# State-space scan on one core: three PSUM banks for the decay arguments, one for y

## The chip, the core and the metric

The kernel runs on one core of a Trainium2 chip. The metric is the device time of one execution in microseconds; a smaller number is better. TensorE (PE) multiplies, ScalarE (ACT) applies functions and copies, VectorE (DVE) does the elementwise work, GpSimd (POOL) builds small operands, and SyncE (SP) issues the transfers.

## The reference

A small vision tower: patch embedding of 64 images into 37 tokens of width 256, then four residual blocks (a selective state-space block, a mixture of experts, a latent attention, a second mixture of experts), each behind a layer norm. The change is in the scan of the first block, which is, cut to what matters:

```python
delta = softplus(x @ W_delta + b_delta)
dA  = exp(delta[..., None] * A)                            # 64 images x 128 channels x 64 states, per token
dBx = delta[..., None] * Bm[:, :, None, :] * x[..., None]
def step(h, inputs):
    dA_t, dBx_t, C_t = inputs
    h = dA_t * h + dBx_t
    y_t = einsum("bdn,bn->bd", h, C_t)
    return h, y_t                                          # 37 steps, one per token
```

## The kernel before

**The state.** The state of one token step is 128 partitions by 4096 words (32 pairs of images by 128 channels). A ring of eight such states lies in SBUF (`slot`). The 37 steps t are worked off in halves: a step has four groups m = 0 to 3 of 1024 words, and each half (m = 0, 1 or m = 2, 3) handles its even group on one path and its odd group on another.

**The even group** (m = 0, 2). DVE multiplies decay and old state (`decay_state`, L1850), PE puts the injected term dBx into PSUM banks 2 and 3 (`inject`, by `inject_rows`, L1088), DVE adds it (`add_injected`, L1869).

**The odd group** (m = 1, 3). DVE writes decay times old state into PSUM banks 4 and 5 (`seed_state`, L1858), PE accumulates the injected term on it (`grow`, also L1088), and ACT copies the two banks to SBUF (`copy_grown`, L1572). The next half's `seed_state` waits for that copy, since it writes the same two banks.

**The decays.** For every four steps (a block; nine of them, b = 0 to 8) PE computes the arguments delta times A as 32 quads, each four matmuls into one bank (`make_quad`, L1081), and ACT exponentiates each quad into the decay slots of the coming block (`exp_quad`, L1548). The quads of block b are spread over 13 group positions of block b-1, from m = 3 of its first step on: two after each even group and three after each odd one (`quads_made`). So a loaded half holds two quads (m even), then the grow and its copy, then three quads (m odd). They use banks 0 and 1 in turn: quad k waits for the exponential of quad k-2. The first exponential of a block overwrites states, and so also waits for DVE's multiplications and seeds of the block's first step, and the first `decay_state` of a block waits for all 32 exponentials.

**The output.** `read_state` (L1121, eight matmul records each) multiplies the state of a half with windows of C that POOL builds. Two steps make one y block, which accumulates in bank 6 or 7 in turn. It waits for the half's add and for its copies. ACT evicts the block (`evict_rows`, L1557), PE transposes it back into the first 128 columns of the same bank (`turn_y`, L1130), and ACT copies the result to y (`copy_y`, L1564).

**Order.** Every engine works its own list in a fixed order written out by hand. PE: inject or grow, then read_state (m even), then turn_y (m = 3 of odd t), then the quads of this position. ACT, at each position: copy_grown (m odd), evict_rows (m = 1 of odd t), copy_y (m = 0 of even t), then the exponentials. DVE: decay, two seeds, add. The semaphores `decay_ps` and `decayed` count quads made and exponentiated; SP's reloads of delta wait on `decay_ps`.

Of the kernel before, what the change touches and what calls it, by code (L numbers as in the profile page):

```python
# [12 lines left out]
P = 128  # L13
# [24 lines left out]
NYB = (L + 1) // 2  # L38
assert NBLK * BLK == L - 1
# [59 lines left out]
def build(nc, small, dense, patches, w_lin, a_rows, up0, dn0, w1, w2, b1, b2, gates_dram, slots,  # L99
          rows_dram, delta_dram, h_dram, gate_dram, out):  # L100
    with ExitStack() as ctx:
# [199 lines left out]
        decay_ps, decayed = sem("decay_ps"), sem("decayed")  # L301
# [3 lines left out]
        y_evicted, y_turned, y_copied = sem("y_evicted"), sem("y_turned"), sem("y_copied")  # L305
# [411 lines left out]

        RANGES = ((0, 9, 0, 4), (9, L, 4, THALF))
# [5 lines left out]
        def _(sp):  # L724
# [54 lines left out]
            def load_delta(b):  # L779

                if b >= 2:
                    sp.wait_ge(decay_ps, QUADS * (b - 1))
# [46 lines left out]
            sp.wait_ge(decay_ps, QUADS * NBLK)  # L829
# [159 lines left out]
        def _(pe):  # L989
# [86 lines left out]
            def make_quad(b, k):  # L1076

                g, r = k // 2, k % 2
                pe.wait_ge(decayed, QUADS * b + k - 1)
                for e in range(4):  # L1080
                    mm = nc.tensor.matmul(ps[:, r, e * BT:(e + 1) * BT], a_stat[64 * r:64 * r + 64, g, e, :],  # L1081
                                          delta_in[b % 2][64 * r:64 * r + 64, g, :], start=True, stop=True)
                mm.then_inc(decay_ps, 1)
# [8 lines left out]
            def inject(t, m):  # L1092

                if m == 0:
                    pe.wait_ge(inject_in[t % INJ], 16 * 9 * (t // INJ + 1))
                pe.wait_ge(added, 2 * t + m // 2)
                inject_rows(t, m, 0, 2, True)
                inject_rows(t, m, 1, 3, True).then_inc(injected, 1)

            def grow(t, m):  # L1100

                for half in range(2):
                    if t >= 1:
                        pe.wait_ge(seeded, 4 * (t - 1) + m - 1 + half + 1)
                    elif m == 3:
                        pe.wait_ge(copied, half + 1)
                    inject_rows(t, m, half, 4 + half, t == 0).then_inc(grown, 1)

            def read_state(t, r):
# [6 lines left out]
                if first and yb >= 2:  # L1116
                    pe.wait_ge(y_copied, yb - 1)
                for j in range(4):
                    quad = r * 4 + j
                    win = t % SLOTS * 256 + quad * 32  # L1120
                    mm = nc.tensor.matmul(ps[32 * j:32 * j + 32, 6 + yb % 2, :], c_win[:, win:win + 32],  # L1121
                                          slot[slot_of(t)][:, quad * 512:(quad + 1) * 512],
                                          start=first, stop=(tp == 1 and r == 1), skip_group_check=True)
                mm.then_inc(read_ps, 1)

            def turn_y(yb):

                pe.wait_ge(y_evicted, yb + 1)
                for x in range(4):
                    mm = nc.tensor.matmul(ps[:, 6 + yb % 2, 0:P], y_rows[yb % 2][:, x * P:(x + 1) * P],  # L1130
                                          S("turn")[:, x * P:(x + 1) * P], start=(x == 0), stop=(x == 3))
                mm.then_inc(y_turned, 1)
# [3 lines left out]
            for k in range(QUADS):  # L1136
                if k < 2:
                    pe.wait_ge(piece_cut, 6 + 2 * k + 1)
                    g, r = k // 2, k % 2
                    for e in range(4):  # L1140
                        mm = nc.tensor.matmul(ps[:, r, e * BT:(e + 1) * BT], a_stat[64 * r:64 * r + 64, g, e, :],
                                              delta_in[0][64 * r:64 * r + 64, g, :], start=True, stop=True)
                    mm.then_inc(decay_ps, 1)
# [314 lines left out]
        def _(act):  # L1458
# [86 lines left out]
            def exp_quad(b, k):  # L1545

                act.wait_ge(decay_ps, QUADS * b + k + 1)
                nc.scalar.activation(decay_slots[b % 2][:, :, 4 * k:4 * k + 4],  # L1548
                                     ps[:, k % 2, :].rearrange("p (e t) -> p t e", e=4),
                                     ACT.Exp).then_inc(decayed, 1)  # L1550

            def evict_rows(yb):

                act.wait_ge(read_ps, 4 * yb + 2)
                if yb >= 2:
                    act.wait_ge(y_turned, yb - 1)
                nc.scalar.activation(y_rows[yb % 2], ps[:, 6 + yb % 2, :], ACT.Copy).then_inc(y_evicted, 1)  # L1557

            def copy_y(yb):

                act.wait_ge(y_turned, yb + 1)
                got = ps[:, 6 + yb % 2, 0:P].rearrange("p (i l) -> p i l", i=NI)
                n = 1 if yb == 0 else 2
                nc.scalar.activation(y3[:, :, max(2 * yb - 1, 0):2 * yb + 1], got[:, :, 2 - n:2],  # L1564
                                     ACT.Copy).then_inc(y_copied, 1)

            def copy_grown(t, m):

                for half in range(2):
                    act.wait_ge(grown, 4 * t + m - 1 + half + 1)  # L1570
                    quad = 2 * m + half
                    nc.scalar.activation(slot[slot_of(t)][:, quad * 512:(quad + 1) * 512], ps[:, 4 + half, :],  # L1572
# [163 lines left out]
        def _(dve):  # L1736
# [106 lines left out]
            def decay_state(t, m):  # L1843

                if m == 0 and (t - 1) % BLK == 0:
                    dve.wait_ge(decayed, QUADS * (block_of(t) + 1))
# [5 lines left out]
            def seed_state(t, m):  # L1852

                now, before = slot[slot_of(t)], slot[slot_of(t - 1)]
                for half in range(2):
                    hs = slice((2 * m + half) * 512, (2 * m + half + 1) * 512)
                    dve.wait_ge(copied, 4 * (t - 1) + m - 1 + 2 + half + 1)
                    nc.vector.tensor_tensor(ps[:, 4 + half, :], now[:, hs], before[:, hs],  # L1858
                                            ALU.mult).then_inc(seeded, 1)

            def add_injected(t, m):
# [3 lines left out]
                if t == 0:  # L1865
                    nc.vector.tensor_copy(now, ps[:, 2:4, :]).then_inc(added, 1)
                else:
                    dve.wait_ge(multed, 2 * (t - 1) + m // 2 + 1)
                    nc.vector.tensor_tensor(now, now, ps[:, 2:4, :], ALU.add).then_inc(added, 1)  # L1869
# [9 lines left out]
            dve.wait_ge(y_copied, NYB)  # L1879
# [351 lines left out]
```

## Time and profile before

| what | value |
|---|---|
| time, median of 3 runs | 1216.77 us (1213.23 to 1216.87) |
| the profiled execution, own time | 1216.49 us |
| its span | 1214.3 us |
| mean granted TensorE clock | 0.862 of full |
| busy over the span | PE 82%, DVE 54%, ACT 42%, POOL 24% |
| the scan | from 154 to 564 us of the span |

Busy shares are over the whole span. An engine's idle time is listed with the work whose end released it. In a timeline, "x8" are eight instructions merged into one row, and the bracket is the idle time before the first of them. The duration of a merged row runs from its first start to its last end, and neighbouring instructions of an engine overlap in part.

### The profile page before, as it was taken

How to read it: one execution, taken by the hardware profiler on the slowest of the kernel's cores; microseconds unless marked ns; L12 is line 12 of the kernel's file. 1: busy time of each engine (PE TensorE's matmuls, PEld its weight loads, DVE VectorE, ACT ScalarE, POOL GpSimd, SP SyncE). 2: the span in 40 equal slices, each digit the busy share in tenths (PEclk: the TensorE clock that was granted, in tenths of full speed). 3: DMA queues.
4: the chain of work that ended last, by engine and by line, in shares of the span. 5: the costliest groups of instructions: out<-in, count | busy, mean ns of one | idle time of the engine just before them, and what ended most of it. 6: DMA issues, size and time to landing. Idle time of an engine off the chain costs nothing.

```text
span 1214.3 us, 17630 instructions
## 1 busy us (share of the span) xinstructions
PE 991.2 (82%) x5925; PEld 614.1 (51%) x5926; DVE 658.1 (54%) x1129; ACT 515.7 (42%) x1028; POOL 295.5 (24%) x361
## 2 busy tenths in 40 slices
PE   8986272777877878765999999998999999559996
PEld 6763230332232333222567777775776666336664
DVE  1544722577676667777535444444876676413332
ACT  1237360766576666662432222224444443223332
POOL 5904901122222222100000000004543541141222
PEclk9998655767677677798989999999999999759999
DMA  5292479212112211116153121100000000342221
GB/s 222 87 335 92 110 211 214 50 44 45 43 27 44 44 26 42 30 38 280 70 218 114 40 73 47 40 0 1 1 1 1 0 1 1 139 160 75 86 78 35
DMA packets 92705, 96.06 MB, mean 79 GB/s; under 512 B 64350, under 2 KB 78687, under 8 KB 90976
## 3 DMA queue, kind: packets, MB, share of 16 engines
q1 hardware_dynamic: 89904, 87.91, 23.7%
q0 software_dynamic: 2736, 7.30, 1.6%
q8 instruction: 39, 0.64, 0.2%
q14 instruction: 26, 0.21, 0.1%
HBM read 61.57 MB, written 34.59 MB: 79 GB/s over the span
## 4 chain that ended last, share of the span: by engine, by line
PE 66%; ACT 14%; DVE 7%; issue 4%; DMA 4%; SPq 4%; POOL 2%; ACTq 0%; DVEq 0%; POOLq 0%
PE ps L524 8%; PE ps L583 7%; PE ps L1121 7%; ACT mem L1548 6%; PE ps L1003 4%; PE ps L1405 4%; PE ps L1421 4%; PE ps L1081 4%; ACT mem L1572 3%; PE ps L1316 3%; PE ps L393 3%; PE ps L1250 3%; PE ps L401 2%; PE ps L1088 2%; PE ps L1130 2%
## 5 line engine op out<-in xcount | busy, mean ns | idle before, releaser
L1548 ACT ACTIVATE mem<-ps 128x512 f32<-128x512 f32 x288 | 160.2, 607 | 104.0 <-PE ps L1081 78.6
L1081 PE MATMUL ps<-mem 64*128 64x128 bf16 x1144 | 106.7, 257 | 98.7 <-ACT mem L1548 96.5
L960 POOL TENSOR_TENSOR mem<-mem,sm 128x296 f32<-128x296 f32 x128 | 87.7, 720 | 361.8 <-ACT mem L1637 319.1
L1081 PEld LDWEIGHTS ps<-mem 64*128 64x128 bf16 x1144 | 63.0, 109 | 195.9 <-ACT mem L1548 166.2
L938 POOL TENSOR_SCALAR mem<-mem,sm 128x16 f32<-128x16 f32 x148 | 92.0, 645 | 274.6 <-PE ps L1121 274.6
L1858 DVE TENSOR_TENSOR ps<-mem 128x512 f32<-128x512 f32 x144 | 93.6, 695 | 61.4 <-ACT mem L1572 61.2
L524 PE MATMUL ps<-mem 128*128 (+1 forms) x384 | 111.6, 422 | 0.6 <-DVE mem L497 0.6
L1121 PE MATMUL ps<-mem 128*32 128x512 f32 x592 | 107.9, 809 | 2.3 <-issue 1.6
L1850 DVE TENSOR_TENSOR mem<-mem 128x1024 f32<-128x1024 f32 x72 | 87.7, 1218 | 35.6 <-ACT mem L1548 35.6
L1572 ACT ACTIVATE mem<-ps 128x512 f32<-128x512 f32 x148 | 82.2, 605 | 58.3 <-PE ps L1088 58.1
L1088 PE MATMUL ps<-mem 64*128 64x512 bf16 x296 | 89.7, 487 | 15.8 <-DVE ps L1858 7.2
L1869 DVE TENSOR_TENSOR mem<-mem,ps 128x1024 f32<-128x1024 f32 x72 | 87.6, 1217 | 27.3 <-PE ps L1088 27.3
L583 PE MATMUL ps<-mem 128*128 128x296 f32 x352 | 99.7, 413 | 2.2 <-DVE mem L646 2.2
L607 ACT ACTIVATE mem<-ps 128x296 f32<-128x296 f32 x88 | 36.7, 417 | 141.9 <-PE ps L524 137.9
L524 PEld LDWEIGHTS ps<-mem 128*128 128x128 f32 x384 | 74.5, 194 | 24.4 <-issue 1.6
L583 PEld LDWEIGHTS ps<-mem 128*128 128x128 f32 x352 | 66.8, 190 | 23.4 <-DVE mem L646 2.6
L646 DVE TENSOR_TENSOR mem<-mem 128x296 f32<-128x296 f32 x88 | 41.1, 467 | 41.8 <-ACT mem L607 39.6
L640 DVE TENSOR_TENSOR mem<-mem 128x296 f32<-128x296 f32 x64 | 29.9, 467 | 52.2 <-ACT mem L607 46.8
L1405 PE MATMUL ps<-mem 128*128 x104 | 51.4, 617 | 7.6 <-issue 7.0
L1003 PE MATMUL ps<-mem 128*128 128x288 f32 x192 | 51.9, 425 | 5.2 <-DMA mem<-in_patches 5.2
L1088 PEld LDWEIGHTS ps<-mem 64*128 64x128 bf16 x296 | 23.7, 107 | 62.8 <-DVE ps L1858 43.3
L431 DVE TENSOR_TENSOR mem<-mem 128x592 f32 (+1 forms) x32 | 25.0, 781 | 49.2 <-ACT mem L418 49.2
(224 smaller groups left out, 1617.5 us busy)
## 6 DMA issues: line engine op xcount, KB each, us to landing
mem<-gates SPq DMA_DIRECT2D x7, 1184.0 KB, 6.0
mem<-in_w SPq DMA_DIRECT2D x2, 4096.0 KB, 17.7
slots<-mem SPq DMA_DIRECT2D x1, 6682.0 KB, 23.8
mem<-slots SPq DMA_DIRECT2D x26, 257.0 KB, 2.7
mem<-in_patches SPq DMA_DIRECT2D x7, 864.0 KB, 4.6
mem<-factor_rows SPq DMA_DIRECT2D x296, 16.0 KB, 1.8
mem<-factor_rows SPq DMA_DIRECT2D x37, 128.0 KB, 2.3
mem<-delta_rows SPq DMA_DIRECT2D x9, 512.0 KB, 4.5
```

What stands on the lines that cost most here:

```text
L524: mm = nc.tensor.matmul(ps[:, bank, 0:CH], w[:, k, row0:row0 + P], xn[:, k, cols], start=(k == 0), stop=(k == HALVES - 1))
L583: mm = nc.tensor.matmul(ps[:, 1 + 2 * cj + m, 0:CH], dn_w[:, j - 2, m * P:(m + 1) * P], hid2[:, b, :], start=(j == 2 and n == nt), stop=(j ...
L938: nc.gpsimd.tensor_scalar(c_win4[:, t % SLOTS * 2 + r, :, w0:w0 + 8].rearrange("p j (x i) -> p j x i", i=2)[:, :, :, i], c_all[:, r * 16:r ...
L960: last = nc.gpsimd.tensor_tensor(kbd[p % 2][:, a, im, :, :], bc(kT[cj][:, a, t0:t0 + L], 1, 8), bc(mask, 2, L), ALU.mult)
L1003: mm = nc.tensor.matmul(ps[:, 2 * j + m, 0:IC * NP], wl[:, f, m * P:(m + 1) * P], xin[:, j, f, :], start=(f == 0), stop=(f == FK - 1))
L1081: mm = nc.tensor.matmul(ps[:, r, e * BT:(e + 1) * BT], a_stat[64 * r:64 * r + 64, g, e, :], delta_in[b % 2][64 * r:64 * r + 64, g, :], sta ...
L1088: return nc.tensor.matmul(ps[:, bank, :], b_in[t % INJ][rows, m, :], dx_in[t % INJ][rows, m, :, :].rearrange("p x n -> p (x n)"), start=st ...
L1121: mm = nc.tensor.matmul(ps[32 * j:32 * j + 32, 6 + yb % 2, :], c_win[:, win:win + 32], slot[slot_of(t)][:, quad * 512:(quad + 1) * 512], s ...
L1405: mm = nc.tensor.matmul(ps[:, 2 + j, 0:HID1], slot_xT[j][:, k, :], w1s[:, k, ds(e * HID1, HID1)], start=(k == 0), stop=(k == 1))
L1548: nc.scalar.activation(decay_slots[b % 2][:, :, 4 * k:4 * k + 4], ps[:, k % 2, :].rearrange("p (e t) -> p t e", e=4), ACT.Exp).then_inc(de ...
L1572: nc.scalar.activation(slot[slot_of(t)][:, quad * 512:(quad + 1) * 512], ps[:, 4 + half, :], ACT.Copy).then_inc(copied, 1)
L1858: nc.vector.tensor_tensor(ps[:, 4 + half, :], now[:, hs], before[:, hs], ALU.mult).then_inc(seeded, 1)
```

## The change

The eight banks are dealt out anew. The quads of decay arguments go round banks 0, 1 and 2; the injected term moves to banks 3 and 4, the grown group to 5 and 6, and y accumulates in bank 7 alone. The transposed y no longer goes back into its own bank but takes a place in the ring of three, in the order in which quads and y blocks come (`RING_AT`). Two semaphores count places instead of quads: `made` (by PE) and `taken` (by ACT, raised by the exponentials and by copy_y). A place waits for the place three before it. On ACT, evict_rows stands ahead of copy_grown at m = 1 of odd t, and copy_y moves from m = 0 of the next step to m = 3 of the same step, behind copy_grown. The first read_state of a y block now waits for the eviction of the block before.

```diff
+DECAY_BANKS = 3
+INJ_BANK, GROW_BANK, Y_BANK = 3, 5, 7
...
+        RING_AT = {}
+        for k in range(QUADS):
+            RING_AT[0, k] = k
+        for t in range(L):
+            for m in range(GROUPS):
+                if m == 3 and t % 2 == 1:
+                    RING_AT["y", t // 2] = len(RING_AT)
+                for b, k in quads_made(t, m):
+                    RING_AT[b, k] = len(RING_AT)
+        RING_AT["y", NYB - 1] = len(RING_AT)
...
             def make_quad(b, k):
-                g, r = k // 2, k % 2
-                pe.wait_ge(decayed, QUADS * b + k - 1)
+                g, r, at_ = k // 2, k % 2, RING_AT[b, k]
+                pe.wait_ge(taken, at_ - DECAY_BANKS + 1)
                 for e in range(4):
-                    mm = nc.tensor.matmul(ps[:, r, e * BT:(e + 1) * BT], a_stat[64 * r:64 * r + 64, g, e, :],
+                    mm = nc.tensor.matmul(ps[:, ring_bank(at_), e * BT:(e + 1) * BT], a_stat[64 * r:64 * r + 64, g, e, :],
...
             def read_state(t, r):
-                if first and yb >= 2:
-                    pe.wait_ge(y_copied, yb - 1)
+                if first and yb >= 1:
+                    pe.wait_ge(y_evicted, yb)
...
             def turn_y(yb):
+                at_ = RING_AT["y", yb]
                 pe.wait_ge(y_evicted, yb + 1)
+                pe.wait_ge(taken, at_ - DECAY_BANKS + 1)
                 for x in range(4):
-                    mm = nc.tensor.matmul(ps[:, 6 + yb % 2, 0:P], y_rows[yb % 2][:, x * P:(x + 1) * P],
+                    mm = nc.tensor.matmul(ps[:, ring_bank(at_), 0:P], y_rows[yb % 2][:, x * P:(x + 1) * P],
...
             for t in range(L + 1):
                 for m in range(GROUPS):
+                    if m == 1 and t % 2 == 1:
+                        evict_rows(t // 2)
                     if t < L and m % 2 == 1:
                         copy_grown(t, m)
-                    if m == 1 and t % 2 == 1:
-                        evict_rows(t // 2)
-                    if t >= 2 and m == 0 and t % 2 == 0:
-                        copy_y(t // 2 - 1)
+                    if t < L and m == 3 and t % 2 == 1:
+                        copy_y(t // 2)
```

## Rows read from the trace of the kernel before

**Rows 1.** Page, part 2: granted TensorE clock in 40 equal slices.
```profile
PEclk9998655767677677798989999999999999759999
```
**Rows 2.** Windows: stretch, length, busy of PE, PEld, DVE, ACT, POOL, clock, DMA.
```profile
287.70:329.09 41.39, 32.40 (x240) 12.90 (x240) 28.82 (x34) 26.71 (x52) 10.34 (x17) 0.71 0.18 39
...
496.50:533.00 36.50, 26.66 (x240) 10.86 (x240) 27.00 (x31) 26.59 (x52) 1.78 (x4) 0.87 0.12 27
533.00:562.00 29.00, 20.41 (x118) 5.75 (x110) 27.85 (x32) 10.95 (x20) 0.20 (x1) 0.94 0.56 211
```
**Rows 3.** Waits from 213 to 563 us: engine, line, releaser, total, times, longest.
```profile
PE ps L1081 <- ACT mem L1548: 86.6, 88, 22.7
ACT mem L1548 <- PE ps L1081: 75.5, 74, 2.2
...
DVE mem L1850 <- ACT mem L1548: 35.6, 8, 4.7
```
**Rows 4.** Timeline, one loaded half at full clock: start, duration, instruction, idle before.
```profile
337.68 1.08 ACT L1548 ACTIVATE mem<-ps 128x512 f32<-128x512 f32 x2 [0.18 <-PE ps L1081]
...
338.33 0.88 PE L1081 MATMUL ps<-mem 64*128 64x128 bf16 x8 [0.37 <-ACT mem L1548]
338.65 1.09 ACT L1572 ACTIVATE mem<-ps 128x512 f32<-128x512 f32 x2
...
339.29 1.30 DVE L1858 TENSOR_TENSOR ps<-mem 128x512 f32<-128x512 f32 x2 [0.32 <-ACT mem L1572]
339.61 1.71 ACT L1548 ACTIVATE mem<-ps 128x512 f32<-128x512 f32 x3
...
340.29 0.28 PE L1081 MATMUL ps<-mem 64*128 64x128 bf16 x2 [1.08 <-ACT mem L1548]
...
340.83 1.06 PE L1121 MATMUL ps<-mem 128*32 128x512 f32 x8
...
341.83 0.41 PE L1081 MATMUL ps<-mem 64*128 64x128 bf16 x8
...
342.26 1.08 ACT L1548 ACTIVATE mem<-ps 128x512 f32<-128x512 f32 x2 [0.94 <-PE ps L1081]
```
**Rows 5.** Timeline of PE, a half at half clock with a turn_y.
```profile
310.39 1.93 PE L1121 MATMUL ps<-mem 128*32 128x512 f32 x8
312.26 0.62 PE L1081 MATMUL ps<-mem 64*128 64x128 bf16 x8
312.66 0.64 PE L1088 MATMUL ps<-mem 64*128 64x512 bf16 x2
313.23 1.96 PE L1130 MATMUL ps<-sm,mem 128*128 128x128 f32 x8
```
**Rows 6.** Timeline of ACT: the first exponentials after each read_state, 301 to 324 us.
```profile
301.08 1.08 ACT L1548 ACTIVATE mem<-ps 128x512 f32<-128x512 f32 x2 [0.94 <-PE ps L1081]
...
306.33 1.08 ACT L1548 ACTIVATE mem<-ps 128x512 f32<-128x512 f32 x2 [1.62 <-PE ps L1081]
...
312.90 1.09 ACT L1548 ACTIVATE mem<-ps 128x512 f32<-128x512 f32 x2 [2.23 <-PE ps L1081]
...
318.18 1.09 ACT L1548 ACTIVATE mem<-ps 128x512 f32<-128x512 f32 x2 [0.73 <-PE ps L1081]
...
323.45 1.08 ACT L1548 ACTIVATE mem<-ps 128x512 f32<-128x512 f32 x2 [1.64 <-PE ps L1081]
```
**Rows 7.** Timeline of DVE: the first decay_state of two blocks.
```profile
285.96 1.23 DVE L1850 TENSOR_TENSOR mem<-mem 128x1024 f32<-128x1024 f32 x1 [4.47 <-ACT mem L1548]
...
327.34 1.23 DVE L1850 TENSOR_TENSOR mem<-mem 128x1024 f32<-128x1024 f32 x1 [4.68 <-ACT mem L1548]
```
**Rows 8.** Timeline of ACT: start of block 1's exponentials, and of a later block's.
```profile
212.13 1.09 ACT L1548 ACTIVATE mem<-ps 128x512 f32<-128x512 f32 x2 [24.63 <-DMA factor_rows<-mem]
...
336.21 1.09 ACT L1548 ACTIVATE mem<-ps 128x512 f32<-128x512 f32 x2 [1.13 <-PE ps L1081]
337.19 0.32 ACT L1564 ACTIVATE mem<-ps 128x128 f32<-128x128 f32 x1
```

More of the change, by code:

```diff
@@ L300, in build @@
         inject_in = [sem(f"inject_in{n}") for n in range(INJ)]
-        decay_ps, decayed = sem("decay_ps"), sem("decayed")
+        made, taken = sem("made"), sem("taken")
         injected, multed, added = sem("injected"), sem("multed"), sem("added")
@@ L781, in load_delta @@
                 if b >= 2:
-                    sp.wait_ge(decay_ps, QUADS * (b - 1))
+                    sp.wait_ge(made, block_taken(b - 2))
                 c0 = (1 + BLK * b) * PAIRS
@@ L827, in _ @@
                     load_delta(t // BLK + 2)
-            sp.wait_ge(decay_ps, QUADS * NBLK)
+            sp.wait_ge(made, block_taken(NBLK - 1))
             sp.wait_ge(h_out, 16)
@@ L1106, in grow @@
                         pe.wait_ge(copied, half + 1)
-                    inject_rows(t, m, half, 4 + half, t == 0).then_inc(grown, 1)
+                    inject_rows(t, m, half, GROW_BANK + half, t == 0).then_inc(grown, 1)
             def read_state(t, r):
@@ L1136, in _ @@
             for k in range(QUADS):
-                if k < 2:
+                if k < DECAY_BANKS:
                     pe.wait_ge(piece_cut, 6 + 2 * k + 1)
@@ L1545, in exp_quad @@
             def exp_quad(b, k):
-                act.wait_ge(decay_ps, QUADS * b + k + 1)
+                at_ = RING_AT[b, k]
+                act.wait_ge(made, at_ + 1)
                 nc.scalar.activation(decay_slots[b % 2][:, :, 4 * k:4 * k + 4],
-                                     ps[:, k % 2, :].rearrange("p (e t) -> p t e", e=4),
-                                     ACT.Exp).then_inc(decayed, 1)
+                                     ps[:, ring_bank(at_), :].rearrange("p (e t) -> p t e", e=4),
+                                     ACT.Exp).then_inc(taken, 1)
             def evict_rows(yb):
@@ L1571, in copy_grown @@
                     quad = 2 * m + half
-                    nc.scalar.activation(slot[slot_of(t)][:, quad * 512:(quad + 1) * 512], ps[:, 4 + half, :],
+                    nc.scalar.activation(slot[slot_of(t)][:, quad * 512:(quad + 1) * 512], ps[:, GROW_BANK + half, :],
                                          ACT.Copy).then_inc(copied, 1)
@@ L1857, in seed_state @@
                     dve.wait_ge(copied, 4 * (t - 1) + m - 1 + 2 + half + 1)
-                    nc.vector.tensor_tensor(ps[:, 4 + half, :], now[:, hs], before[:, hs],
+                    nc.vector.tensor_tensor(ps[:, GROW_BANK + half, :], now[:, hs], before[:, hs],
                                             ALU.mult).then_inc(seeded, 1)
@@ L1865, in add_injected @@
                 if t == 0:
-                    nc.vector.tensor_copy(now, ps[:, 2:4, :]).then_inc(added, 1)
+                    nc.vector.tensor_copy(now, ps[:, INJ_BANK:INJ_BANK + 2, :]).then_inc(added, 1)
                 else:
                     dve.wait_ge(multed, 2 * (t - 1) + m // 2 + 1)
-                    nc.vector.tensor_tensor(now, now, ps[:, 2:4, :], ALU.add).then_inc(added, 1)
+                    nc.vector.tensor_tensor(now, now, ps[:, INJ_BANK:INJ_BANK + 2, :], ALU.add).then_inc(added, 1)
             for t in range(L):
```

35 lines of the change are left out of this document (20 added, 15 removed).

## The prediction, made before the changed kernel was run

> **What bounds the kernel now.** I read the clock and the windows first, then the waits of the scan, then the timeline of single halves. The clock over the span shows that the scan (slices 5 to 18) is the only long stretch well below full clock [rows 1]. A block in the middle takes 41.4 us although DVE is busy for 28.8 of it and ACT for 26.7, and PE for 32.4 at a mean clock of 0.71 [rows 2]: no engine is full. The last stretch, 533 to 562 us, has no quads left; DVE is busy for 27.9 of its 29 us there, so DVE alone would do a half in about 3.5 us. The waits say who holds whom: PE's quads wait 86.6 us for exponentials (22.7 of it one wait at the start), and the exponentials wait 75.5 us for quads [rows 3]. Two engines that wait for each other are a ring that is too short.
>
> The timeline of a half shows the loop [rows 4]. ACT does the two exponentials of the even position (337.68), the two copies (338.65), three exponentials (339.61). PE's third odd quad starts only at 340.29, after 1.08 us idle, when the first of those three has ended, because it is two places behind it. Everything else on PE is queued behind this quad: the injection, read_state (340.83, 1.0 us), and the next two quads (341.83). Their exponentials start at 342.26, after ACT stood idle for 0.94 us. The half takes 342.26 - 337.68 = 4.58 us.
>
> **The change, part by part.**
>
> Third bank. The third odd quad then waits for the second even exponential (ends near 338.8) instead of the first odd one. It can be made while ACT copies. Injection waits for the add before, which DVE has long done. Next in the queue is read_state, which really needs the half's second copy (ends 338.65 + 1.09 = 339.74). So the new loop is: copies end, about 0.1 us to start read_state (an estimate), 1.43 us from the start of read_state to the start of the next exponential (342.26 - 340.83), 0.97 us for two exponentials (the spacing of two, 338.65 - 337.68), 1.09 for the copies: 3.6 us. Against this stand ACT's own seven instructions at 0.485 us, 3.4 us, and DVE's 3.5. All three are close; I take 3.6. A full-clock half gains 1.0 us of its 4.58.
>
> At half clock PE is slower: from read_state's start to ACT's start it is 312.90 - 310.39 = 2.5 us [rows 5, 6], so the loop becomes 0.1 + 2.5 + 0.97 + 1.09 = 4.7 us. PE's own work there is 1.87 for read_state, 0.40 for two quads, 0.57 for the grow, at most 1.3 for three quads (the 0.43 that four matmuls would take one behind the other), and 0.57 for the injection: 4.7 too.
>
> Now one block, between the exponentials behind the read_states [rows 6]. Five intervals: 4.58 (like the half above), then 306.33 - 301.08 = 5.25, 6.57, 5.28 and 5.27, and 3.9 from 323.45 to the end of the last exponential, which releases DVE at 327.34 [rows 7]. With the same clock in each place they become: 3.6; 4.3 (read_state partly slow, its lag estimated at 2.1 us, between 1.43 and 2.5); 5.2 (4.7 and an eviction of 0.49); 4.6 (below); 4.3; 3.5. The saving is 1.0 + 0.95 + 1.4 + 0.7 + 1.0 + 0.4 = 5.4 us. At full clock throughout: 3.6, 3.6, 4.1, 3.7, 3.6, 3.5, a saving of 8.7. ACT's idle time there is 0.94 + 1.62 + 2.23 + 0.73 + 1.64 = 7.2, and 8.3 with the smaller waits between; 0.2 in each of five halves stays, so by this count it is 7.3. I take 8.
>
> All blocks. Of the 75.5 us, seven waits of 1.1 to 2.0 us, 9.5 together, are the first exponential of a block, set by another chain; one of them is the 1.13 before 336.21 [rows 8]. The other 66 are eight times block 2's 8.3, so block 2 stands for all eight: the same clock gives 8 x 5.4 = 43 us, full clock 8 x 8 = 64.
>
> Block start. Between the last exponential (327.3) and the next first one (336.2) DVE works its decays and seeds without a gap and then PE its turn_y: 8.9 us that the third bank does not touch. At full clock turn_y would take about half of its 1.9 [rows 5], 0.9 us sooner in each of 8 blocks: 7 us more in the full-clock case only, 71 in all.
>
> y in the ring. turn_y waits for the place three before it, a quad whose exponential ACT does before the copies of this half: no delay beyond the eviction. The quads behind it see the same distance of three, and the third of them waits for copy_y. copy_y now sits on ACT ahead of three exponentials and waits for turn_y, and the next quad is behind turn_y on PE anyway, so ACT would be idle there: its 0.32 us [rows 8] falls into that gap. At half clock the chain is read_state 1.87, quads 0.40, grow 0.57, turn_y 1.9, and at the then full clock 0.63 and 0.3: 5.7 us from one read_state to the next where it was 6.36, which is the 0.7 above. If the cover is gone, it is 18 x 0.32 = 6 us.
>
> Eviction ahead of the copies, one bank for y. It delays the copies by 0.49 us in every fourth half, and read_state and the seeds with them; that is in the 5.2 and 4.1 above. Before, it stood ahead of the exponential on which PE waited, so it cost as much. read_state's new wait for the eviction is covered by the wait for the copies, which ACT does later. If it were not covered, 18 x 0.49 = 9 us.
>
> Start and tail. The exponentials of block 0 run faster with three banks, but block 1's first one waits 24.63 us for the transfers of the factor rows and starts at 212.13 [rows 8]: nothing gained there. From 533 us on DVE is full: nothing either. SP, whose transfers for a step fit twice into its 7 us, only sees its semaphores renamed.
>
> One rule speaks against a gain. The Trainium skill ("TensorE: Matmul & The Clock Gate", HAM oscillation) reports a kernel in which adding PSUM double-buffering gave no further gain. By it the sum would be 0; the 86.6 us in rows 3 say that here the banks are waited for, so I go by the rows.
>
> **Which clock.** In the full-clock stretches PE stood idle in gaps of 0.3 to 1.1 us [rows 4], and the clock fell between them; in the last stretch, at 3.5 us a half, PE is busy for 70% and the clock 0.94 [rows 2]. Block 8 had the old pattern and 0.87. With the same work in 3.6 instead of 4.58 us PE is denser, so I expect the clock to rise from 0.71, not all the way. I take a little under the middle of 43 and 71, since block 8 with its 0.87 has less to give: 54 us. The sum is made on the profiled 1216.5, which is 0.3 below the median of the runs: 1216.5 - 54 = 1162.5, say 1163.
>
> **Rivals.**
> 1. PE takes over. The clock stays at half over most of the exponentials, PE's 4.7 us a half and its turn_y bind, and 10 to 40 us are saved: 1176 to 1206. For it: PE is already busy for 32.4 of 41.4 us. Against it: that is at 0.71.
> 2. Full clock all through, or the copies leave DVE free sooner than worked out: over 71 us, below 1145. Its cap is the 75.5 us plus the 7 of turn_y: 1134.
> 3. Not faster: the clock drops. If it is at half throughout, 6.5 loaded halves at 4.7 us, and one turn_y of 1.9 us that binds, are 32.5 us from the first to the last exponential, where a block needed 41.4 - 8.9 = 32.5 before. Block 8 took 36.5 us [rows 2] and not 41.4, and would lose 5: 1216.5 + 5 = 1221. It decides once the scan's clock falls below about 0.55. The Trainium skill ("TensorE: Matmul & The Clock Gate", A second HAM failure mode) describes a kernel whose cycling through PSUM banks made the clock swing; no row here shows that more banks do so.
> 4. The change does not do what it says: the third quad is held by something else. The release at the end of an exponential [rows 4] speaks against it. 1213 to 1221.
>
> **How the numbers follow.** The forecast has 0.73, rival 1 0.14, rival 2 0.06, rival 3 0.04, rival 4 0.03. A measurement of this kernel tells 0.3% (3.7 us) from no change. Faster: 0.73 + 0.14 + 0.06 and a little, 0.93; the same 0.04; slower 0.03. The likeliest case alone spans 1145 (71 saved) to 1174 (43). The range for 8 in 10 reaches past both into rivals 2 and 1: 1143 to 1182; the 0.2 us a half that separates the floors of ACT and DVE from my 3.6 (8 to 10 us over some 48 halves) lies in it.
>
> **What would show it.** Right: a full-clock half of 3.5 to 3.8 us; the waits between L1081 and L1548 down from 86.6 and 75.5 to below 45 each; blocks of 33 to 37 us; block 1 still starting near 212 us; L1121 directly behind L1572; the tail still 29 us; clock of the scan above 0.75. Wrong: L1548 still waits near 1 us in full-clock halves, or L1572 and L1858 wait instead, or the clock of the blocks stays near 0.5 to 0.6 and PE is busy all through.

## The result and the profile after

| | before | after |
|---|---|---|
| time, median (4 runs each) | 1215.42 us (1213.23 to 1216.87) | 1156.51 us (1151.05 to 1159.42) |
| ratio | | 0.951, 95% interval 0.947 to 0.955 |
| profiled execution: span | 1214.3 us | 1153.4 us |
| mean granted clock over the span | 0.862 | 0.910 |
| from the first exponential of block 1 to the last copy_y | 351.8 us (212.1 to 563.9) | 287.9 us (208.7 to 496.6) |

The change makes the kernel 59 us faster; 1163 was forecast, with a range of 1143 to 1182. In the profiles the stretch of the last row is 63.9 us shorter. The rest of the difference of the spans, 60.9 us, is 3.4 us less ahead of it and 6.4 us more behind it. Neither belongs to the change. 3.0 us of the earlier start were there at 131 us, ahead of every changed line. Behind the scan the changed kernel took 656.8, 654.9 and 653.5 us in three profiled executions, and kernels of the experiments with the same code there took 649.3 to 656.1. So the stretch of the last row is the finer measure for what follows. "The stretch" below means this one, and a block's period is the distance of two blocks' last exponentials.

In the changed kernel the lines are: make_quad L1102, inject and grow L1109, read_state L1142, turn_y L1153, exp_quad L1572, evict_rows L1581, copy_y L1589, copy_grown L1597, decay_state L1875, seed_state L1883, add_injected L1894.

First the clock, as in [rows 1], and then windows of the changed kernel, as in [rows 2]: one block, the tail, then a block start and the loaded part behind it.

```profile
PEclk9999656898898998989999999979999998579999
```

```profile
299.03:332.74 33.71, 25.56 (x240) 11.00 (x240) 28.52 (x32) 26.04 (x53) 12.04 (x17) 0.90 0.22 48
465.71:494.80 29.09, 19.84 (x110) 5.41 (x110) 27.86 (x32) 11.07 (x21) 0.20 (x1) 0.94 0.55 210
...
265.70:276.30 10.60, 8.18 (x50) 3.24 (x51) 10.60 (x13) 4.10 (x8) 3.15 (x5) 0.68 0.36 77
...
276.30:299.00 22.70, 17.40 (x192) 7.68 (x189) 17.80 (x20) 21.87 (x45) 8.82 (x13) 1.00 0.16 34
```

A block takes 33.7 us here where it took 41.4, with the same work. The last two rows split a block. At its start VectorE is busy throughout (10.60 of 10.60) and the clock is at 0.68. In the loaded part, up to the block's last exponential, the clock is 1.00 and ScalarE is listed as busy for 21.9 of 22.7 us. The same two parts before the change:

```profile
327.30:338.00 10.70, 9.88 (x58) 3.12 (x50) 10.66 (x13) 4.38 (x10) 2.38 (x6) 0.62 0.36 77
338.00:368.50 30.50, 22.17 (x189) 9.19 (x190) 18.13 (x20) 22.30 (x44) 7.73 (x11) 0.78 0.11 25
```

The block start is as long as it was (10.6 us against 10.7); the gain is in the loaded part (22.7 against 30.5). The waits of the changed kernel, 210 to 510 us (engine, line, releaser, total, times, longest), against [rows 3]:

```profile
DVE mem L1875 <- ACT mem L1572: 25.0, 8, 3.1
...
PE ps L1102 <- ACT mem L1572: 9.8, 39, 0.3
ACT mem L1572 <- PE ps L1102: 9.7, 20, 0.7
...
ACT mem L1589 <- PE ps L1153: 6.8, 8, 1.2
...
PE ps L1102 <- ACT mem L1589: 5.7, 8, 0.7
```

The 75.5 us that exponentials waited for quads are 9.7, and no matmul of a quad waits longer than 0.3 us for an exponential. The last row is a new wait: once a block a quad waits 0.7 us for copy_y, the other user of the ring. The timeline of a loaded half, as in [rows 4]:

```profile
277.27 1.09 ACT L1597 ACTIVATE mem<-ps 128x512 f32<-128x512 f32 x2
...
278.23 2.75 ACT L1572 ACTIVATE mem<-ps 128x512 f32<-128x512 f32 x5
278.47 1.07 PE L1142 MATMUL ps<-mem 128*32 128x512 f32 x8 [0.41 <-issue]
279.12 1.21 DVE L1894 TENSOR_TENSOR mem<-mem,ps 128x1024 f32<-128x1024 f32 x1
279.47 0.41 PE L1102 MATMUL ps<-mem 64*128 64x128 bf16 x8
...
280.55 0.77 PE L1102 MATMUL ps<-mem 64*128 64x128 bf16 x6 [0.25 <-ACT mem L1572]
280.87 1.09 ACT L1597 ACTIVATE mem<-ps 128x512 f32<-128x512 f32 x2
```

Read it from the copies. They end at 277.27 + 1.09 = 278.36, and read_state starts 0.11 us later. Before, the third odd quad stood between the two. The five exponentials (three odd, two even) are one row now, the next copies follow at once, and the half takes 280.87 - 277.27 = 3.60 us where it took 4.58.

That row is not free of idle time, though. A timeline that begins at 279.86 shows its two even exponentials by themselves:

```profile
279.90 1.08 ACT L1572 ACTIVATE mem<-ps 128x512 f32<-128x512 f32 x2
```

Instructions of this size start 0.48 us apart when the next one is ready (the copies at 277.27, the exponential behind the two at 278.23). After three odd ones from 278.23 on, the fourth could start at 279.66. It starts at 279.90, 1.43 us behind read_state's start at 278.47, the same lag as in [rows 4]. So the seven instructions by themselves would need 7 x 0.477 = 3.34 us, 0.24 us of the half are a wait for the even quads, and the loop of the prediction sets the half: 0.11 + 1.43 + 0.97 + 1.09 = 3.60.

Once a block, with turn_y in the half, it goes less well:

```profile
287.70 1.16 PE L1153 MATMUL ps<-sm,mem 128*128 128x128 f32 x8
...
288.54 1.09 ACT L1597 ACTIVATE mem<-ps 128x512 f32<-128x512 f32 x2
289.50 0.35 ACT L1589 ACTIVATE mem<-ps 128x128 f32<-128x128 f32 x1
...
289.90 0.28 PE L1102 MATMUL ps<-mem 64*128 64x128 bf16 x2 [0.71 <-ACT mem L1589]
...
290.44 1.06 PE L1142 MATMUL ps<-mem 128*32 128x512 f32 x8
...
291.87 1.08 ACT L1572 ACTIVATE mem<-ps 128x512 f32<-128x512 f32 x2 [0.59 <-PE ps L1102]
```

The third odd quad waits for copy_y, three places before it, and read_state is queued behind this quad. It starts 0.8 us after the copies' end instead of 0.1, and from one even pair to the next are 4.30 us (287.57 to 291.87). It is the old fault once more, in one half of a block.

### The profile page after: what moved, and what is told of

It is laid out like the page before. It is cut to its first block, busy times and chain, and to the rows that moved or that the text cites. A ratio compares the mean times of both kernels' runs of the same rounds, so it can differ in the third digit from the quotient of the medians.

```text
span 1153.4 us, 17650 instructions
## 1 busy us (share of the span) xinstructions
PE 935.1 (81%) x5925; PEld 597.4 (52%) x5926; DVE 657.2 (57%) x1129; ACT 508.3 (44%) x1028; POOL 305.0 (26%) x361
## 4 chain that ended last, share of the span: by engine, by line
PE 64%; ACT 12%; DVE 9%; issue 6%; SPq 4%; DMA 4%; another core or an unknown queue 0%; POOL 0%; ACTq 0%; DVEq 0%; POOLq 0%
PE ps L526 8%; PE ps L585 8%; PE ps L1142 6%; ACT mem L1572 5%; PE ps L1024 4%; PE ps L1428 4%; PE ps L1444 4%; PE ps L1339 3%; PE ps L1273 3%; PE ps L395 3%; PE ps L1102 3%; PE ps L403 3%; SPq L783 2%; ACT mem L1597 2%; PE ps L1285 2%
## 5 line engine op out<-in xcount | busy, mean ns | idle before, releaser
L1572 ACT ACTIVATE mem<-ps 128x512 f32<-128x512 f32 x288 | 154.0, 637 | 42.9 <-DMA factor_rows<-mem 30.3
L959 POOL TENSOR_SCALAR mem<-mem,sm 128x16 f32<-128x16 f32 x148 | 102.7, 716 | 203.5 <-PE ps L1142 203.5
L1102 PE MATMUL ps<-mem 64*128 64x128 bf16 x1140 | 92.0, 230 | 53.6 <-ACT mem L1572 44.3
L1102 PEld LDWEIGHTS ps<-mem 64*128 64x128 bf16 x1140 | 56.0, 99 | 121.6 <-ACT mem L1572 102.4
L1883 DVE TENSOR_TENSOR ps<-mem 128x512 f32<-128x512 f32 x144 | 93.5, 694 | 42.1 <-ACT mem L1597 41.6
L526 PE MATMUL ps<-mem 128*128 (+1 forms) x384 | 108.6, 413 | 0.6 <-DVE mem L499 0.6
L1597 ACT ACTIVATE mem<-ps 128x512 f32<-128x512 f32 x148 | 82.4, 609 | 54.0 <-PE ps L1109 53.8
L1142 PE MATMUL ps<-mem 128*32 128x512 f32 x592 | 87.3, 663 | 22.1 <-issue 13.6
L1109 PE MATMUL ps<-mem 64*128 64x512 bf16 x296 | 76.7, 421 | 31.5 <-DVE ps L1883 21.6
L1875 DVE TENSOR_TENSOR mem<-mem 128x1024 f32<-128x1024 f32 x72 | 87.7, 1218 | 25.0 <-ACT mem L1572 25.0
L1894 DVE TENSOR_TENSOR mem<-mem,ps 128x1024 f32<-128x1024 f32 x72 | 87.4, 1213 | 1.2 <-PE ps L1109 0.7
L648 DVE TENSOR_TENSOR mem<-mem 128x296 f32<-128x296 f32 x88 | 41.1, 467 | 41.8 <-ACT mem L609 39.6
L1109 PEld LDWEIGHTS ps<-mem 64*128 64x128 bf16 x296 | 21.3, 96 | 71.3 <-DVE ps L1883 54.3
```

Source lines behind the costliest of these rows:

```text
L526: mm = nc.tensor.matmul(ps[:, bank, 0:CH], w[:, k, row0:row0 + P], xn[:, k, cols], start=(k == 0), stop=(k == HALVES - 1))
L959: nc.gpsimd.tensor_scalar(c_win4[:, t % SLOTS * 2 + r, :, w0:w0 + 8].rearrange("p j (x i) -> p j x i", i=2)[:, :, :, i], c_all[:, r * 16:r ...
L1102: mm = nc.tensor.matmul(ps[:, ring_bank(at_), e * BT:(e + 1) * BT], a_stat[64 * r:64 * r + 64, g, e, :], delta_in[b % 2][64 * r:64 * r + 6 ...
L1109: return nc.tensor.matmul(ps[:, bank, :], b_in[t % INJ][rows, m, :], dx_in[t % INJ][rows, m, :, :].rearrange("p x n -> p (x n)"), start=st ...
L1142: mm = nc.tensor.matmul(ps[32 * j:32 * j + 32, Y_BANK, :], c_win[:, win:win + 32], slot[slot_of(t)][:, quad * 512:(quad + 1) * 512], start ...
L1875: nc.vector.tensor_tensor(now[:, gs], now[:, gs], before[:, gs], ALU.mult).then_inc(multed, 1)
```

## The experiments

Each kernel was timed beside the kernel before. "The stretch" is from its profiled execution, and the period is the mean of seven.

| kernel | time, us (range) | ratio to before, 95% interval | stretch, us | period, us | clock in the stretch |
|---|---|---|---|---|---|
| before | 1215.4 | 1 | 351.8 | 41.2 | 0.75 |
| changed | 1156.5 (1151.1 to 1159.4) | 0.947 to 0.955 | 287.9 | 33.3 | 0.92 |
| changed, second | 1155.7 (1150.3 to 1157.0) | 0.942 to 0.954 | 290.6 | 33.2 | 0.89 |
| changed, third | 1156.4 (1151.5 to 1161.8) | 0.947 to 0.954 | 289.5 | 33.4 | 0.91 |
| ring2 | 1228.9 (1225.4 to 1229.6) | 1.006 to 1.014 | 356.6 | 41.8 | 0.77 |
| evict_late | 1161.0 (1159.2 to 1161.6) | 0.950 to 0.957 | 292.1 | 33.5 | 0.89 |
| before_filler | 1220.4 (1211.8 to 1225.7) | 1.001 to 1.006 | 351.8 | 41.4 | 0.79 |
| before_filler4 | 1211.4 (1199.8 to 1218.4) | 0.992 to 0.998 | 344.1 | 40.4 | 0.86 |
| short_exp | 1135.3 (1131.3 to 1138.5) | 0.928 to 0.940 | 270.2 | 30.3 | 0.89 |
| turn_late | 1158.0 (1155.1 to 1161.1) | 0.947 to 0.955 | 290.1 | 33.2 | 0.89 |
| feed_first | 1159.6 (1156.0 to 1164.9) | 0.948 to 0.960 | 292.8 | 33.6 | 0.91 |
| warm_start | 1153.2 (1147.8 to 1156.8) | 0.943 to 0.954 | 283.4 | 32.5 | 0.95 |
| start_all | 1151.1 (1147.0 to 1157.7) | 0.943 to 0.951 | 284.0 | 32.3 | 0.93 |

**ring2: the third place alone.** One line of the changed kernel.

```diff
-DECAY_BANKS = 3
+DECAY_BANKS = 2
```

> The changed kernel with DECAY_BANKS = 2: everything moved as in the change, but two places in the ring. If the third place is what gains, the third odd quad waits again for the first odd exponential, a full-clock half is again near 4.6 us, the waits between quads and exponentials are again 70 to 90 us, the scan's clock is again near 0.7, and the time is 1208 to 1225 us. If the gain came from where the eviction and copy_y now stand on ScalarE, or from y leaving its second bank, it stays near 1160.

Measured: 1228.9 us, a stretch of 356.6. The waits, 206 to 570 us:

```profile
PE ps L1102 <- ACT mem L1572: 83.1, 88, 22.3
ACT mem L1572 <- PE ps L1102: 70.6, 61, 2.2
```

The old waits are back, and with them all of the time. So the whole gain comes from the third place. The rest of the change alone, in a ring of two, costs 0.6 to 1.4%. That is 12.8 us in the medians and 4.8 in the stretch. That copy_y then holds one place of only two may be the reason; no run shows it.

**evict_late: the eviction's place.** The changed kernel with the two calls on ScalarE in the old order.

```diff
-                    if m == 1 and t % 2 == 1:
-                        evict_rows(t // 2)
                     if t < L and m % 2 == 1:
                         copy_grown(t, m)
+                    if m == 1 and t % 2 == 1:
+                        evict_rows(t // 2)
```

> The changed kernel with evict_rows behind copy_grown again. The loop (copies, read_state, two quads, two exponentials) holds the eviction either way, since read_state of a new y block now waits for it: within 5 us of the changed kernel's 1156.5. If the eviction's place ahead of the copies mattered, this is 9 us slower (18 evictions by 0.49 us) or more.

Measured: 1161.0 us, 4.5 above the changed kernel, inside the 5 us that "no difference" allowed. The stretch is 292.1 against 287.9 to 290.6. The two ratios' intervals overlap; so a loss of a few microseconds is possible but not shown, and 9 us do not fit either number. In its trace the even pairs around an eviction lie 4.13 us apart in six of eight blocks, against 4.08 in the changed kernel, so the order by itself costs 0.05 us there.

**before_filler and before_filler4: the clock without the ring.** The kernel before, with extra matmuls ahead of the third odd quad: two, then four.

```diff
                             if k == 0:
                                 pe.wait_ge(delta_loaded[b % 2], 16 * (b // 2 + 1))
+                            if m % 2 == 1 and (b, k) == quads_made(t, m)[-1]:
+                                pe.wait_ge(added, 2 * t + (m + 1) // 2)
+                                for _ in range(2):                # 4 in before_filler4
+                                    nc.tensor.matmul(ps[:, 2, :], a_stat[0:64, 0, 0, :],
+                                                     a_stat[0:64, 0, :, :].rearrange("p e n -> p (e n)"),
+                                                     start=True, stop=True, skip_group_check=True)
                             make_quad(b, k)
```

> The kernel before with two extra matmuls (64x512, results unused) in each odd position, ahead of the third odd quad, where TensorE stands idle for about 1 us waiting for the exponential; the ring stays at two. It tells the clock's part of the gain from the ring's. If the denser TensorE by itself keeps the clock at full level, the scan's clock rises from 0.7 to above 0.85, full-clock halves stay at 4.6 us, and the slow halves and slow turn_y are gone: about 3.2 us a block and 0.9 at each block start, 1188 to 1200. If the clock does not follow, or the extra matmuls cost what the clock gives, it is 1210 to 1225. If the clock alone were the cause of the gain, it would come near 1160.

> before_filler with four extra matmuls in each odd position instead of two. With two, TensorE was busier (80% against 76% of the stretch) and the clock only rose from 0.75 to 0.79. At full clock four fit into the wait of 1.1 us (0.9 us); at half clock they take 1.7 and cost about 0.4 a half. If work in the gap lifts the clock as a shorter loop does, the loaded stretch goes to full clock and the time falls to 1188 to 1200. If the clock stays near 0.75, it rises to 1220 to 1235, and the clock's part of the gain stays unproved by this way.

Neither came out as either theory had it. Two extra matmuls lifted the clock of the stretch only to 0.79, and the time was 0.1 to 0.6% above the kernel before. Four lifted it to 0.86, and the stretch fell to 344.1 us. The times (1211.4, 0.2 to 0.8% less than before) missed the 1188 to 1200 of the first theory, and lie under the 1220 to 1235 of the second. But before_filler4 has blocks of 38.3 to 42.8 us. Windows over two neighbouring ones:

```profile
318.33:356.67 38.34, 30.68 (x276) 12.06 (x268) 28.86 (x32) 26.82 (x52) 11.82 (x16) 0.96 0.20 42
356.67:399.49 42.82, 37.23 (x276) 14.75 (x268) 28.91 (x33) 26.83 (x52) 10.68 (x16) 0.76 0.18 38
```

With two banks a block at nearly full clock (0.96) takes 38.3 us. The last block of the kernel before took 38.3 too (494.7 to 533.0, at a clock of 0.85). By these blocks the clock's part is 41.2 - 38.3 = 2.9 us of a block, and the third place gives the other 38.3 - 33.3 = 5.0: over eight blocks 23 and 40 us of the 63.9. The split is rough. Put together from the shortest interval of each kind in the traces with two banks, the loaded part is 28.5 us, where its mean was 32.1 before and is 24.3 in the changed kernel; by this count the clock has 29 us and the third place 34. And the clock did not rise by itself: ring2, with every other edit, had 0.77. So its rise hangs on the third place too. Whether the shorter waits of TensorE or its denser work brought it, no run separates.

**short_exp: what bounds the changed kernel.**

```diff
-                nc.scalar.activation(decay_slots[b % 2][:, :, 4 * k:4 * k + 4],
-                                     ps[:, ring_bank(at_), :].rearrange("p (e t) -> p t e", e=4),
+                n = BT if b < 2 else BT // 2
+                nc.scalar.activation(decay_slots[b % 2][:, 0:n, 4 * k:4 * k + 4],
+                                     ps[:, ring_bank(at_), :].rearrange("p (e t) -> p t e", e=4)[:, 0:n, :],
```

> The changed kernel with the exponentials of blocks 2 to 8 over half of their columns: this leaves out half of the decays of those blocks. It asks what bounds the changed kernel in its loaded halves. ScalarE's work there falls from 3.6 to about 2.4 us a half. If ScalarE alone was the bound, the halves fall to VectorE's 3.5 us, 0.1 us in each of some 42 halves plus the longer halves with an eviction, 0.5 us in 14 more, and the stall of 0.6 before the fourth exponential goes: 12 to 18 us in all. If the loop from the copies through read_state and two quads (3.6 us as worked out) binds with it, only the exponentials' own shortening inside the loop counts and less than 8 us are gained.

Measured: 20.4 us less in the stretch than the changed kernel's second run, on the same chip, above the 12 to 18 of the first theory. A loaded half of it (exp_quad is L1573, copy_grown L1598, add_injected L1895):

```profile
276.60 1.07 PE L1142 MATMUL ps<-mem 128*32 128x512 f32 x8 [0.41 <-issue]
277.25 1.22 DVE L1895 TENSOR_TENSOR mem<-mem,ps 128x1024 f32<-128x1024 f32 x1
...
278.03 0.66 ACT L1573 ACTIVATE mem<-ps 128x256 f32<-128x256 f32 x2 [0.70 <-PE ps L1102]
...
278.57 1.09 ACT L1598 ACTIVATE mem<-ps 128x512 f32<-128x512 f32 x2
...
280.73 1.22 DVE L1895 TENSOR_TENSOR mem<-mem,ps 128x1024 f32<-128x1024 f32 x1
281.20 0.66 ACT L1573 ACTIVATE mem<-ps 128x256 f32<-128x256 f32 x2 [0.70 <-PE ps L1102]
```

From read_state to ScalarE are 1.43 us, exactly as in [rows 4]; the loop is 281.20 - 278.03 = 3.17 us; and VectorE goes at its own pace, 280.73 - 277.25 = 3.48. The first theory does not hold: the halves fell below VectorE's 3.5, to 3.17, and ScalarE now stands idle for 0.70 us in each. What fell is the loop, by 0.43 us, and that is what the two exponentials inside it lost: 0.97 before, now 0.54 (278.57 - 278.03). Over the five such intervals of each of the seven shortened blocks that is 15 us, and the last half of a block, with no read_state behind it, gives 1.06 us more (3.53 to 2.47), 7 in all; the block starts give about 2 us back. So the second theory had the mechanism, but its "less than 8 us" was too small. The loop bounds the changed kernel's loaded halves at 3.60 us, VectorE stands 0.1 us behind it, and ScalarE with its 3.34 us of work 0.26. That VectorE's 3.48 did not hold the 3.17 back fits the longer intervals of a block, 3.66 and 3.87 us, in which it can catch up.

**turn_late, warm_start, feed_first and start_all: the block start.** What is left is mostly there. turn_late puts turn_y and copy_y behind the first two quads of a block (and their place in the ring with them). `starts_block` names the position, m = 3, at which a block's first quads stand:

```diff
-                    if t < L and m == 3 and t % 2 == 1:
+                    if t < L and m == 3 and t % 2 == 1 and not starts_block(t, m):
                         turn_y(t // 2)
                     if t < L:
                         for b, k in quads_made(t, m):
...
                             make_quad(b, k)
+                        if starts_block(t, m):
+                            turn_y(t // 2)
```

> The changed kernel with turn_y and copy_y behind the first two quads and exponentials of a block instead of ahead of them, at the block starts alone (8 places); elsewhere as in the change. If ScalarE bounds the changed kernel from the first to the last exponential of a block without a gap, what comes off the block start (a turn_y of 1.5 to 2.0 us and a copy_y of 0.3) comes off the time: 8 x 2 = 16 us, 1140 to 1146. If the exponentials after the first two are held by read_state and VectorE at the block start instead, less than 5 us are gained.

Measured: no gain (1158.0). The rival was right. The timeline of ScalarE (exp_quad L1580, copy_y L1597, copy_grown L1605), behind a last exponential that released VectorE at 270.08:

```profile
277.73 1.10 ACT L1580 ACTIVATE mem<-ps 128x512 f32<-128x512 f32 x2
278.89 0.32 ACT L1597 ACTIVATE mem<-ps 128x128 f32<-128x128 f32 x1
280.53 1.08 ACT L1580 ACTIVATE mem<-ps 128x512 f32<-128x512 f32 x2 [1.32 <-PE ps L1108]
281.50 1.09 ACT L1605 ACTIVATE mem<-ps 128x512 f32<-128x512 f32 x2
```

The first pair comes 7.7 us after the last exponential of the block before instead of 9.2, but the second pair only after 10.5 (10.6 in the changed kernel): its quads still stand behind turn_y, injection and read_state on TensorE.

warm_start adds work where TensorE waits at the block start:

```diff
+                    if t < L and m in (1, 2) and quads_made(t, 3)[:1] == [(block_of(t) + 1, 0)]:
+                        at_ = RING_AT["y", t // 2]
+                        pe.wait_ge(taken, at_)
+                        for _ in range(5 if m == 1 else 1):
+                            nc.tensor.matmul(ps[:, ring_bank(at_), :], a_stat[0:64, 0, 0, :],
+                                             a_stat[0:64, 0, :, :].rearrange("p e n -> p (e n)"),
+                                             start=True, stop=True, skip_group_check=True)
                     if t < L and m % 2 == 0:
                         inject(t, m)
```

> The changed kernel with six extra matmuls (64x512, results unused) where TensorE waits for VectorE at each block start: five ahead of the first grow, one ahead of the second injection. If the half clock of the block start is due to TensorE's idling there and the extra work ends it, turn_y takes 1.1 instead of 2.0 us and read_state 1.0 instead of 1.9, the first exponentials come 1 us sooner or more in each of 8 blocks, and the time falls by 7 to 10 us. If the clock does not follow such work, as in before_filler, the time stays within 4 us, or rises by what the extra matmuls take.

A block of it, and the same kind of turn_y as in [rows 5], there 1.96 us long:

```profile
267.83:299.93 32.10, 24.83 (x246) 10.58 (x246) 28.25 (x33) 26.16 (x53) 9.13 (x17) 1.00 0.23 51
```

```profile
274.13 1.16 PE L1153 MATMUL ps<-sm,mem 128*128 128x128 f32 x8
```

The clock did follow this work: the block runs at 1.00 throughout and takes 32.1 us. The periods alternate, though (32.7, 32.1, 32.7, ...); in every other block the clock is 0.80 up to the first exponential. The stretch is 283.4 us, 7.2 below the second run of the changed kernel beside it. In the times 2.5 us are left of it, less than the 7 to 10 expected, and the runs do not separate it from nothing.

feed_first is turn_late with the quads of every even position ahead of read_state:

```diff
+                    if t < L and m % 2 == 0:
+                        for b, k in quads_made(t, m):
+                            make_quad(b, k)
                     if t < L and m % 2 == 1:
                         grow(t, m)
                     if t >= 1 and m == 0:
                         read_state(t - 1, 1)
```

> turn_late, and on top of it the quads of an even position are made ahead of read_state instead of behind it, everywhere. turn_late gained nothing, since the second pair of a block's quads still stood behind turn_y, the injection and read_state at the block start (its exponentials began at 280.5 us, 10.5 after the last of the block before, against 10.7 in the changed kernel). If that queue is what holds the block start, the second pair now follows the first at once, ScalarE works without a gap from 7.7 us after the last exponential on, and a block falls from 33.3 to about 30.7 us: 18 to 22 us less, 1134 to 1140. If VectorE's chain at the block start holds it, less than 5 us.

Neither theory held. The time is 1159.6 us, so less than 5 us were gained, but not for VectorE's sake. A loaded half of it (copy_grown L1608, exp_quad L1583):

```profile
286.67 1.08 ACT L1608 ACTIVATE mem<-ps 128x512 f32<-128x512 f32 x2 [0.33 <-PE ps L1115]
287.64 2.56 ACT L1583 ACTIVATE mem<-ps 128x512 f32<-128x512 f32 x5
```

ScalarE's copies now wait 0.33 us for the grow, which stands behind read_state, and a half takes 282.81 to 286.67, 3.86 us. The same five exponentials take 2.56 us here and 2.75 in the changed kernel: with the even quads made in time, the wait inside the row is gone. The block start did get shorter: the copies of the third half came 10.9 us after the last exponential in the mean of seven blocks, against 11.5. The next kernel keeps the one and drops the other.

start_all is turn_late and warm_start together, with the quads ahead of read_state only in the one position that follows a block's first two:

```diff
+                    second = m == 0 and 2 <= t < L and starts_block(t - 1, 3)
+                    if second:
+                        for b, k in quads_made(t, m):
+                            make_quad(b, k)
```

> Three edits of the block start on the changed kernel: the extra matmuls of warm_start, turn_y and copy_y behind the first two quads as in turn_late, and the next two quads ahead of read_state as in feed_first, but at this one place. feed_first lost 0.26 us in every loaded half (3.86 instead of 3.60, its copies waited 0.33 for the grow) and gained 1.1 at each block start; here only the gain should be left. VectorE's three halves after the last exponential, 10.4 us, are the floor of the block start, so a block falls from 33.3 us to about 32.0: 8 x 1.3 = 10 us less than the changed kernel in the stretch from the first exponential of block 1 to the last copy_y, 279 to 283 us. If warm_start's gain and the order's gain are the same microseconds, it is no better than warm_start's 283.

The changed kernel was timed a second and a third time beside these. Of the first of the two:

> The changed kernel once more, as the measure for the others of this call. From the first exponential of block 1 to the last copy_y 287 to 291 us; the time 1150 to 1160.

and of the other:

> The changed kernel once more, as the measure for start_all: 1150 to 1160 us, 287 to 292 of it from the first exponential of block 1 to the last copy_y.

start_all has the lowest time of the kernels that leave nothing out, 1151.1 us against 1156.4 beside it (ratios to before 0.943 to 0.951 and 0.947 to 0.954, so the intervals still overlap), and a stretch of 284.0 against 289.5. A block at full clock takes 31.5 us:

```profile
271.00:302.53 31.53, 24.90 (x246) 10.77 (x246) 27.96 (x32) 26.04 (x53) 11.68 (x17) 1.00 0.23 52
```

but its periods range from 31.5 to 33.8, and the mean, 32.3, is hardly better than warm_start's 32.5. The 10 us expected were 5.5. So the order at the block start is worth at most 0.6 us a block (31.5 against 32.1), and the clock there as much or more.

## Why the prediction was right

**The loop.** The step "the third odd quad waits for the exponential two places behind it, and everything else is queued behind that quad" was the cause, shown by ring2. The new loop was put at 3.6 us with 0.1 us from the copies to read_state; it is 3.60 with 0.11. The lag of 1.43 us from read_state to ScalarE held in the changed kernel and in short_exp. ScalarE's floor was put at 3.4 (it is 3.34) and VectorE's at 3.5 (3.48), both under the loop, as they turned out.

**The sum.** For full clock throughout the loaded part 64 us were worked out without turn_y's 7. The stretch shrank by 63.9: that case came, without the 7. The mis-sized step was the clock. I took 54 us as a point somewhat under the middle between an unchanged clock (43) and full clock everywhere (71). In fact the clock did not settle between the two; it split by place: 1.00 in the loaded part, 0.62 to 0.80 from the last exponential of a block to the next first one, where turn_y stayed near 2.0 us in five of seven blocks (1.16 and 1.56 in the others). By that split the sum is 64, and by the medians 59 were measured. The rest is the variation outside the stretch.

That the 64 came out so exactly is in part luck. For block 2 the intervals at full clock gave a saving of 8.7 us and the idle time 7.3, and 8 was taken between them. Measured, the part from a block's first exponential to its last is 7.85 us shorter in the mean. And "block 8 took 36.5 us" was a misreading: its window in [rows 2] begins 1.8 us after the block, which took 38.3. That bears on rival 3 and on how far 54 was put under the middle, not on the mechanism.

**Clock's share.** The two cases differed by 21 us for the loaded part; before_filler4's block at 0.96 gives 2.9 us a block, 23 us, and the count by the shortest intervals 29. Both are near it, but the first comes from blocks of one profiled execution in which extra matmuls ran as well.

**The y block.** Here a term was put at nothing that is not nothing. The prediction saw that the third quad behind turn_y waits for copy_y, and had copy_y's time fall into idle time of ScalarE. But what waits is that quad, and read_state behind it. The interval with turn_y was put at 3.7 us at full clock and takes 4.30, in every one of the eight blocks: 5 us in all. It takes 0.6 of the 8.7 us by which the prediction's intervals shrink, and the 8 that was taken instead about covers it. At the block starts copy_y waits for turn_y 8 times, 6.8 us in all, without visible loss: the first exponential comes 8.2 to 9.3 us after the last one, 9.0 in the mean, against 8.9 to 9.3 and 9.1 before. The interval with the eviction takes 4.08 us where 4.1 was predicted. read_state's wait for the eviction shows in no row of the waits.

**Start and tail.** Block 1 starts when the transfers land, and the tail is 29.1 us, as predicted.

**The rivals.** PE takes over: no, TensorE is busy for 17.4 of 22.7 us in the loaded part. The clock drops: no. With three banks in the ring the clock of the loaded part is 1.00, with two it was 0.78. The case given beside that rival (the Trainium skill, "TensorE: Matmul & The Clock Gate", A second HAM failure mode) puts the swings down to short idle times of TensorE between groups of matmuls as it cycles through the banks. The traces here agree with it: with two banks TensorE waited for about 1.1 us in a full-clock half, with three for no longer than 0.41 us in an ordinary one. That these waits alone held the clock down is not shown: before_filler4 filled them with extra matmuls and had 0.76 to 0.96. Nor is it a rule against more banks. The report that double-buffering gained nothing further in a kernel (the Trainium skill, "TensorE: Matmul & The Clock Gate", HAM oscillation) does not carry over: here one more bank is 72 us (ring2 against the changed kernel).

**Open.** What a place for y outside the ring of the quads would bring in the half with turn_y, which no run tried; why the clock at some block starts rises with the extra matmuls and at others does not; why ring2 is slower than the kernel before; whether evict_late's 4.5 us are real.

## What to carry to other kernels

When two engines wait for each other in turn, look at what is queued behind the waiting instruction. Here one matmul group of 0.2 us waited for a bank, and read_state, the injection and the next quads waited with it, so one more bank gave 34 to 40 of the scan's 352 us without any work taken away, and the clock, which rose with it, 23 to 29 more. Free the bank where a long accumulation holds two and needs one. A short-lived result can take a place in the same ring, but count it: the quad three places behind copy_y waited 0.7 us, and read_state with it.

An engine that is listed as busy without a gap need not be the bound. Compare the spacing of its instructions with their number: ScalarE had 3.34 us of work in a half of 3.60, and the 0.24 us between were inside one merged row.

Before an edit of the order, follow the second instruction as well as the first: turn_late brought the first pair of exponentials forward by 1.5 us and the second not at all. And making quads ahead of read_state everywhere cost in the loaded halves more than it gained at the 8 block starts.

## What the runs showed of the hardware

With the same matmuls in the stretch, 216.6 us of busy TensorE in 287.9 had a clock of 0.92, and 268.6 in 351.8 had 0.75, nearly the same share (75 and 76%). Busy time counts longer at the lower clock, so the share by itself did not tell the two apart. Extra work lifted the clock in one place (warm_start: a block at 1.00) and hardly in another (before_filler: 0.75 to 0.79).

ScalarE's exponentials and copies of 128x512 took 0.60 us each by themselves but started 0.48 us apart when queued: a group of five ran in 2.56 us (feed_first) and a group of two in 1.09. The 2.75 us of the changed kernel's five contain the wait shown above. Exponentials of 128x256 started 0.26 to 0.28 us apart (short_exp). A sum that uses the mean of one instruction (607 to 637 ns in the groups of the pages) would have put ScalarE's seven at 4.2 to 4.5 us a half and missed that 3.6 was possible.
